# A graph network on one core: the edge loop's fill in another order, edge one-hots compared in bf16 with the tile innermost, Wq and Wk by chunks

## What is computed

```
L0: q, k, v = x@Wq+bq, x@Wk+bk, x@Wv+bv          # 8 heads of 64
    attention over the nodes, masked by the adjacency of the edges, softmax over the queries (axis 1)
    @Wo + bo, layernorm, relu(h@W1+b1)@W2+b2, layernorm
L1: h   = mish(concat(x[src], x[dst], edge_attr) @ W1 + b1)     # 4096 x 512
    m   = mish(h @ W2 + b2)                                     # 4096 x 512
    agg = segment_sum(m, dst);  u = mish(concat(x, agg)@W3 + b3);  u@W4 + b4;  layernorm
L2: two graph convolutions 512 -> 128 -> 512 with a normalised adjacency
L3: x@W_self.T + mean over neighbours(x)@W_neigh.T + bias, layernorm
```

## Time and profile before

| | |
|---|---|
| three runs | 254.29, 254.63, 255.37 us; median 254.63 |
| profiled execution | 255.16 us, its span 253.4 us, mean granted TensorE clock 0.977 |
| busy us (share of the span) | PE 235.5 (93%), PEld 189.6 (75%), DVE 153.9 (61%), ACT 121.6 (48%), POOL 5.6 (2%) |
| chain that ended last | PE 82%, DVE 8%, issue 4%, ACT 4%, POOL 1% |
| largest lines on it | L625 33%, L610 12%, L432 8%, L441 5%, L488 4% |

### The profile page before, as it was taken

How to read it: one execution, slowest core, us unless ns; L and a number is a source line. 1 busy time by engine, 2 the same in 40 slices (tenths; PEclk the granted TensorE clock), 3 DMA queues, 4 the chain that set the end, 5 groups by cost and what they waited for, 6 DMA issues and landing times.

```text
span 253.4 us, 3283 instructions
## 1 busy us (share of the span) xinstructions
PE 235.5 (93%) x1269; PEld 189.6 (75%) x1269; DVE 153.9 (61%) x266; ACT 121.6 (48%) x221; POOL 5.6 (2%) x17
## 2 busy tenths in 40 slices
PE   7998999997998499999999999999999998999980
PEld 3967789764765378888888888888888887986760
DVE  3977875336877335585675856758568355264625
ACT  0415399779267614553654735647455343150000
POOL 0000100001000000000000000000000000000001
PEclk9999999999999679999999999999999999999996
DMA  6999983501930000004505031040000000000001
GB/s 214 319 415 414 406 319 132 168 0 35 281 101 0 0 0 0 3 0 134 197 3 166 0 111 60 0 166 0 0 3 0 0 0 0 3 0 0 3 0 43
DMA packets 12991, 23.39 MB, mean 92 GB/s; under 512 B 920, under 2 KB 3888, under 8 KB 12848
## 3 DMA queue, kind: packets, MB, share of 16 engines
q1 hardware_dynamic: 12336, 22.81, 25.7%
q10 hardware_dynamic: 640, 0.37, 0.6%
HBM read 22.92 MB, written 0.26 MB: 91 GB/s over the span
## 4 chain that ended last, share of the span: by engine, by line
PE 82%; DVE 8%; issue 4%; ACT 4%; POOL 1%; POOLq 0%; DVEq 0%
PE bank L625 33%; PE bank L610 12%; PE bank L432 8%; PE bank L441 5%; PE bank L488 4%; PE bank L635 3%; PE bank L636 3%; PE bank L451 2%; ACT C L281 2%; DVE Sbf L829 2%; DVE Dbf L829 2%; PE bank L421 1%; PE bank L646 1%; PE bank L463 1%; PE bank L415 1%
## 5 line engine op out<-in xcount | busy, mean ns | idle before, releaser
L625 PE MATMUL bank<-W2hi,Hhi 128*128 128x512 f32 x128 | 51.1, 399 | 4.2 <-issue 4.2
L625 PE MATMUL bank<-W2lo,Hhi 128*128 128x512 f32 x128 | 50.9, 398 | 0.0
L625 PE MATMUL bank<-W2hi,Clo 128*128 128x512 f32 x128 | 50.8, 397 | 0.0
L365 ACT ACTIVATE Mhi<-M 128x512 fp32r<-128x512 f32 x32 | 20.2, 632 | 50.6 <-DVE M L933 50.6
L938 DVE TENSOR_TENSOR Mlo<-M,Mhi 128x512 fp32r<-128x512 f32 x32 | 22.1, 689 | 24.4 <-ACT M L366 24.4
L933 DVE TENSOR_TENSOR M<-bank,b2r 128x512 f32<-128x512 f32 x32 | 22.0, 687 | 17.8 <-PE bank L625 9.2
L625 PEld LDWEIGHTS bank<-W2hi,Hhi 128*128 128x128 f32 x128 | 24.7, 193 | 9.8 <-issue 4.6
L625 PEld LDWEIGHTS bank<-W2hi,Clo 128*128 128x128 f32 x128 | 24.7, 193 | 5.2
L625 PEld LDWEIGHTS bank<-W2lo,Hhi 128*128 128x128 f32 x128 | 24.7, 193 | 5.2
L358 ACT ACTIVATE Hhi<-C 128x512 fp32r<-128x512 f32 x32 | 20.0, 624 | 14.7 <-DVE C L919 14.4
L924 DVE TENSOR_TENSOR Clo<-C,Hhi 128x512 fp32r<-128x512 f32 x32 | 22.0, 688 | 6.6 <-ACT C L359 6.5
(11 more groups left out here) (178 smaller groups left out, 315.9 us busy)
## 6 DMA issues: line engine op xcount, KB each, us to landing
F<-in_L_gnn_W SPq DMA_DIRECT2D x2, 2048.0 KB, 13.3
W1raw<-in_L_gnn_W SPq DMA_DIRECT2D x1, 2048.0 KB, 20.9
W<-in_L_gnn_W SPq DMA_DIRECT2D x1, 2048.0 KB, 8.9
Wq<-in_L_gnn_Wq SPq DMA_DIRECT2D x2, 512.0 KB, 5.0
Wk<-in_L_gnn_Wk SPq DMA_DIRECT2D x2, 512.0 KB, 7.7
Wv<-in_L_gnn_Wv SPq DMA_DIRECT2D x1, 1024.0 KB, 11.8
ea<-in_edge_attr SPq DMA_DIRECT2D x1, 1024.0 KB, 12.5
Wo<-in_L_gnn_Wo SPq DMA_DIRECT2D x1, 1024.0 KB, 15.3
```

What stands on the lines that cost most here:

```text
L365: act.activation(Mhi[:, t, :], M[:, t, :], ACT.Mish)
L625: done = mm(ST2[t][:, :], x[:, c, e], w[:, c, :], start=c == 0 and i == 0, stop=c == KC - 1 and i == 2)
```

## The change

Four things are changed.

1. The one-hots. POOL fills a table `numbers` (128 x 128 nodes x 32 tiles, bf16) with the node number; DVE casts the ids to bf16 and compares in that layout, so that in `Dbf` and `Sbf` the 32 tiles lie next to each other for each node. The PE's operands `[:, :, t]` take every 32nd element. All 32 matmuls of `count_edges` stand behind V.
2. Wq and Wk are loaded in four chunks of rows each, and `features_as_loaded` multiplies a chunk into all four quarters as it arrives.
3. Ahead of the fill: edge step 5 moves ahead of the last part of F2's product; ACT's `W2hi` moves behind step 11; DVE's four pieces of `W2lo` are spread; `xw` (y plus a bias row) moves back; the load of W1raw goes behind three rows.
4. The fill. ACT and DVE take their work in another order, and the wait for the late banks moves into `second_layer`: six reads for tiles 0 and 1, eight for tiles 2 and 3.

```
+            pool.iota(numbers, pattern=[[1, N], [0, ET]], base=0, channel_multiplier=0,
+                      allow_small_or_imprecise_dtypes=True).then_inc(S["numbered"], 1)
...
-            for ids, one in ((dcol, Dbf), (scol, Sbf)):
-                v.tensor_tensor(one, ids[:, :].unsqueeze(2).to_broadcast([P, ET, N]),
-                                iota_row[:, :].unsqueeze(1).to_broadcast([P, ET, N]), ALU.is_equal).then_inc(S["onehot_bf"], 1)
+            v.tensor_copy(dcol_bf[:, :], dcol[:, :]).then_inc(S["ids_bf"], 1)
+            v.tensor_copy(scol_bf[:, :], scol[:, :]).then_inc(S["ids_bf"], 1)
+            dve.wait_ge(S["ids_bf"], 2)
+            dve.wait_ge(S["numbered"], 1)
+            for ids, one in ((dcol_bf, Dbf), (scol_bf, Sbf)):
+                v.tensor_tensor(one, ids[:, :].unsqueeze(1).to_broadcast([P, N, ET]), numbers, ALU.is_equal).then_inc(S["onehot_bf"], 1)
...
-                        done = mm(quarter(b, i), by_edge[:, tile_of(g, i), :], ident_bf[:, :], start=True, stop=True)
+                        done = mm(quarter(b, i), by_edge[:, :, tile_of(g, i)], ident_bf[:, :], start=True, stop=True)
...
-            for h in range(2):
-                pe.wait_ge(S[f"wq_in{h}"], 16)
-                features_by(bank[2], 0, (2 * h, 2 * h + 1), Wq, xT, KC, S["q_done"] if h else None)
+            def features_as_loaded(banks, w, arrived, signal):
+
+                per = KC // len(banks)
+                for c in range(KC):
+                    pe.wait_ge(S[f"{arrived}{c}"], 16)
+                    for j in range(KC):
+                        done = mm(quarter(banks[j // per], j), w[:, c, P * j:P * (j + 1)], xT[:, c, :],
+                                  start=c == 0 and j % per == 0, stop=c == KC - 1 and j % per == per - 1)
+                        if c == KC - 1 and j % per == per - 1:
+                            done.then_inc(signal, 1)
...
-                    done = mm(bank[0][:, 0:N], Dbf[:, t, :], Sbf[:, t, :], start=t == 0, stop=t == ET - 1)
+                    done = mm(bank[0][:, 0:N], Dbf[:, :, t], Sbf[:, :, t], start=t == 0, stop=t == ET - 1)
...
-            pe.wait_ge(S["onehot_bf"], 2)
-            count_edges(range(8))
             pe.wait_ge(S["qk_ready"], 2 * KC)
...
             nodes_by(bank[3], xT, Wv, S["v_done"])
-            count_edges(range(8, ET)).then_inc(S["ct_done"], 1)
+            pe.wait_ge(S["onehot_bf"], 2)
+            count_edges(range(ET)).then_inc(S["ct_done"], 1)
...
-            edge_term(range(3, 5))
+            edge_term(range(3, 6))
             for h in range(2):
                 columns_by((bank[1], bank[2]), ffT, F2, h, range(FC - 2, FC), 0, FC - 1).then_inc(S["f2_done"], 1)
 
-            edge_term(range(5, RING_STEPS - 1))
+            edge_term(range(6, RING_STEPS - 1))
...
                     if g >= 1:
                         pe.wait_ge(S["z2_read"], GT * (g - 1) + t + 1)
+                    else:
+                        pe.wait_ge(S["late_read"], 6 if t < 2 else 8)
...
             pe.wait_ge(S["w2_lo"], KC)
-            pe.wait_ge(S["late_read"], 2 * KC)
```

More of the change, by code:

```diff
@@ L63, in gnn_kernel @@
         scol = sb("scol", [P, ET], I32)
+        dcol_bf = sb("dcol_bf", [P, ET], BF16)
+        scol_bf = sb("scol_bf", [P, ET], BF16)
         Ahat = sb("Ahat", [P, N])
@@ L115, in gnn_kernel @@
         EAThi, EATlo = chunks(first["EAThi"], PAIRS), chunks(first["EATlo"], PAIRS)
-        Dbf, Sbf = chunks(other["Dbf"], ET), chunks(other["Sbf"], ET)
+        Dbf, Sbf, numbers = (other[n].rearrange("p (n t) -> p n t", t=ET) for n in ("Dbf", "Sbf", "numbers"))
         W1hi, W1lo = chunks(other["W1hi"], 2 * KC), chunks(other["W1lo"], 2 * KC)
@@ L204, in _ @@
             sp.dma_start(xs[:, :], a["x"]).then_inc(S["x_in"], 16)
-            for h in range(2):
-                sp.dma_start(Wq[:, :, D // 2 * h:D // 2 * (h + 1)], w_view(a["L0_gnn_Wq"])[:, :, D // 2 * h:D // 2 * (h + 1)]).then_inc(S[f"wq_in{h}"], 16)
-            for h in range(2):
-                sp.dma_start(Wk[:, :, D // 2 * h:D // 2 * (h + 1)], w_view(a["L0_gnn_Wk"])[:, :, D // 2 * h:D // 2 * (h + 1)]).then_inc(S[f"wk_in{h}"], 16)
+            for c in range(KC):
+                sp.dma_start(Wq[:, c, :], a["L0_gnn_Wq"][P * c:P * (c + 1), :]).then_inc(S[f"wq_in{c}"], 16)
+            for c in range(KC):
+                sp.dma_start(Wk[:, c, :], a["L0_gnn_Wk"][P * c:P * (c + 1), :]).then_inc(S[f"wk_in{c}"], 16)
             load_row("L0_gnn_bo")
@@ L216, in _ @@
             sp.dma_start(F1, w_view(a["L0_gnn_W1"])).then_inc(S["f1_in"], 16)
-            sp.dma_start(W1raw, w_view(a["L1_gnn_W1"][0:2 * D, :])).then_inc(S["w1_in"], 16)
             for name in EARLY_ROWS[4:]:
                 load_row(name)
+            sp.dma_start(W1raw, w_view(a["L1_gnn_W1"][0:2 * D, :])).then_inc(S["w1_in"], 16)
             sp.wait_ge(S["pre_done"], ST_UNIT)
@@ L347, in _ @@
             features_high(3)
-            edge_term_out(range(3))
+            edge_term_out(range(RING_STEPS))
             act.wait_ge(S["w2_in"], 16)
             act.activation(W2hi[:, :, :], W2raw, ACT.Copy).then_inc(S["w2_hi"], 1)
-            edge_term_out(range(3, KC * PAIRS - 3))
+            edge_term_out(range(RING_STEPS, RING_STEPS + 1))
             def hidden(g, j):
@@ L366, in message @@
                 act.activation(M[:, t, :], M[:, t, :], ACT.Mish).then_inc(S["m_hi"], 1)
-            for j in range(3):
+            for j in range(KC):
                 hidden(0, j)
[L370 to L377, removed]
+            edge_term_out(range(RING_STEPS + 1, KC * PAIRS))
+            for j in range(KC):
+                hidden(1, j)
             for g in range(G):
@@ L888, in _ @@
             v.tensor_copy(Cn[:, :], bank[4][:, N:2 * N]).then_inc(S["graph_ready"], 1)
+            dve.wait_ge(S["nx_ready"], 2)
+            chain(v.tensor_tensor(xw[:, :], y[:, :], r("L0_gnn_b2"), ALU.add))
             xb = r("L0_gnn_be2")
@@ L901, in _, with w2_low @@
             out_halves(xT_flat, xs_banks, S["nT_done"], 2, S["nT_ready"])
-            dve.wait_ge(S["w2_hi"], 1)
-            for c in range(KC):
-                v.tensor_tensor(W2lo[:, c, :], W2raw[:, c, :], W2hi[:, c, :].bitcast(F32), ALU.subtract).then_inc(S["w2_lo"], 1)
+            def w2_low(cs):
+                dve.wait_ge(S["w2_hi"], 1)
+                for c in cs:
+                    v.tensor_tensor(W2lo[:, c, :], W2raw[:, c, :], W2hi[:, c, :].bitcast(F32), ALU.subtract).then_inc(S["w2_lo"], 1)
             dve.wait_ge(S["ab_done"], 1)
@@ L946, in one_hot @@
                                 iota_row[:, :].unsqueeze(1).to_broadcast([P, GT, N]), ALU.is_equal).then_inc(S["m_oh"], 1)
[L948 to L955, removed]
+            for j in range(KC):
+                z1_out(0, j)
+            w2_low((2,))
+            for j in range(KC):
+                hidden_low(0, j)
+                z1_out(1, j)
+                if j == 0:
+                    w2_low((3,))
+            for j in range(KC):
+                hidden_low(1, j)
             for g in range(G):
```

15 lines of the change are left out of this document (7 added, 8 removed).

## The result

The changed kernel takes **258.9 us** (median of four runs, 258.07 to 259.85); the kernel before, on the same chip, 254.53. The ratio is 1.0167, 95% interval 1.0123 to 1.021: it is slower by 4.4 us, where 249.5 was forecast. The profiled execution took 258.64, its span is 256.8 us, the mean granted clock 0.977.

A forecast was written before the change was run, and what follows sets the result against it. The PE, busy 93% of the span, bounds the kernel where it waits or runs slow. -6.94 + 0.38 + 0.1 + 1.35 = -5.1 takes 255.16 to 250.05, median 249.5; range 247.6 to 253.4 (0.84).

The forecast's parts named there:

- Fill: Between `first_layer` and `second_layer`: the 4.19 us hole goes entirely, and the slow clock with it saves 2.75: -6.94 us.
- a wait in its place: Rival at the hole: `hidden_low(0,3)` or late z2 sums make a new wait, say 1.5 us: 251.0; chance 0.12.
- something misread: Rival at the hole: something misread holds the PE to 85 us anyway, only costs stay: 255 to 256; chance 0.04.
- Ring: Edge terms behind the second feed-forward product: step 5 ahead of F2's last part delays the PE's transposes: +0.38 us.
- W1raw at nothing: W1raw's load, 2.0 us later behind three rows, covered by 1.76 us idle ahead of step 1: 0 to 0.24, taken 0.
- Front, +0.1: Q, K and scores: K's last chunk closes all four quarters together, so scores start at 14.9, not 14.82: +0.1 us.
- cover for Wv: Wv's load behind four more issues, 0.1 us of cover before V: nothing to +1.9 us, taken as nothing.
- the table rival: Rival at the start: VectorE's identity waits for POOL's new iota, everything 3.2 us later: 252.7; chance 0.05.
- +1.35: Count behind V: strided moving reads at 0.115 us each, count ends at 23.35, its two products at 25.2: +1.35 us.
- the upper bound of 0.23: Most a strided moving read in the count would cost, from a record reading 512 columns: 0.23 us each, +5.0 us.
- That rival: Rival in the count: moving reads four times slower, +5.0 us, total -1.5, so 253.1; chance 0.16.
- the rival with both operands slow: Rival in count and one-hot transposes: both operands slow; at four times today's cost +7.9 us, 262.5; chance 0.08.

The follow-up runs named there:

- run 11: Kernel before with only the reordered fill, plus the load of W1raw issued behind the bias rows: 248.63 us.
- run 1: Changed kernel with the one-hots of the kernel before, all 32 count matmuls still behind V: 249.29 us.
- run 2: Changed kernel with GpSimd's table iota waiting until VectorE has made its identity: 255.67 us.
- run 5: Kernel of run 1 with W1raw issued ahead of the bias rows again: 249.31 us.
- run 6: Kernel of run 5 with the edge steps as before, two ahead of the first hidden product, not three: 249.01 us.
- run 12: Kernel before with the reordered fill, plus Wq and Wk by chunks and all count matmuls behind V (kernel of run 6 again): 249.03 us.
- run 7: Changed kernel with both identities made by `tensor_tensor` in place of `tensor_scalar`, the iota where the change put it: 256.05 us.
- run 8: Kernel of run 1 with 6 x 16 probe matmuls ahead of the count, moving operand at steps of 2 to 64 bytes: one run, 264.63 us.
- run 4: Changed kernel with only Sbf, the count's moving operand, in the new strided layout and Dbf as before: 257.75 us.
- run 3: Changed kernel with only Dbf, the count's stationary operand, in the new strided layout and Sbf as before: 252.48 us.

## Why the prediction was wrong, point by point

**Fill: right.** -7.24 in the traces against -6.94, hole and slow clock both; alone it gives 6.9 us by the medians, 7.2 by the spans (253.4 to 246.2). The slow clock had cost 3.01 rather than the 2.75 worked out from its 14 matmuls. The two rivals in it (a wait in its place, something misread) didn't occur; the slack on VectorE was 0.66 for 0.6.

**Ring: right.** +0.38 forecast, +0.56 to 0.57 measured, by the cause named (fewer steps ahead of ACT at the end). W1raw at nothing came true by luck: in the changed kernel the late front hid the load, and ACT never waited for it. The cover that was named is real but short: 1.0 us of waiting cost nothing in run 11, 2.1 us cost 0.9 in run 1. And the load was not 2.0 us later: it had landed at 33.6 before, and came at 36.3 (run 11), 36.98 (run 1) and 37.6 (changed kernel).

**Front, +0.1: right as to K's copies** (in run 2, with Q and K at the times of before, the scores start at 14.75 on PE's timeline, as before), too low in its cover for Wv. "A load that spends 11.8 us on its way is waiting for the bytes ahead of it" is borne out in part: issued 1.6 us later it spent 10.5 on its way instead of 11.8. What was missed is that with 0.1 us of cover every late landing of Wv counts (runs 2, 5, 6 and 12, and 11 with halves).

**The step that failed first: "Against: the identity's `tensor_scalar` shows 0.29 and a `tensor_tensor` of the same shape 0.28", and with it the 0.05 for the table rival.** Equal durations were taken as evidence that the identity uses no mode that the iota could block. They are none: the `tensor_scalar` took 0.29 in the kernel before and 4.17 beside the iota, run 7's `tensor_tensor` 0.29 beside it. Price: 3.2 forecast for that rival, 3.49 in the chain of the changed kernel. The iota took 4.17 us and not the 3.2 scaled from the small ones, the identity ended 3.88 later (5.41 against 1.24 + 0.29), and V started 3.49 later. Runs 2 and 7 win back 3.2 and 2.9.

**The second: "+1.35", the moving read at 0.115 us.** It was taken as twice the packed price from an f32 record with twice the bytes per column. The bytes that matter are those from column to column, 64 here, and the flat part of the curve in run 8 was reached: 217 to 218 ns alone (runs 4 and 8), 229 with the stationary operand strided too, the upper bound of 0.23. That bound came from a packed record with four times the columns, and no row had a strided read: that it fits so well is luck. That rival had 0.16, with +5.0 for its read; +6.38 was measured. The missing 1.4 is the clock, which no case had: 1.71 + 1.53 for the two products behind the count, instead of 1.84. Without it, 7.34 + 1.84 - 4.20 = +4.98. Runs 3 and 4 put both parts on the moving side; the rival with both operands slow fell (Sbf's transposes went from 0.45 to 0.50 to 0.52 per 8, not by a factor).

**The structure of the chances.** The two failures were rivals, with prices close to what came, but each was priced alone against a forecast that held the rest. With both, -6.94 + 0.48 + 5.0 + 3.2 = +1.7 would have been slower than before; their conditions had nothing to do with each other, but both were guesses at an edit that the trace of before could not show. With fill and ring right, the error is these two and the clock: 3.49 + (6.38 - 1.35) = 8.5 of the 9.4 us between forecast and result. Between the profiled executions it is 8.5 of 8.6 (258.64 - 250.05); the other 0.8 is the step from profiled to median, taken as -0.5 and found to be +0.26.

## What to carry to other kernels

A layout chosen so that one engine writes fast is read by another. Of the steps tried, keep the moving operand of a bf16 matmul within 4 bytes from column to column (58 ns, against 115 at 8 bytes), and let only a stationary operand be strided where its load is hidden. Keep a long GpSimd instruction (the iota, 4.17 us) away from the short VectorE operations on which the start depends, or write those in a form that it does not block; their duration when alone doesn't tell which form that is. And a bundle of edits can hide a clean gain of 7 us under a loss of 10: price each alone before keeping them together, since here the reordered fill alone was the whole gain.

## What the runs showed of the chip that was not expected

- The granted clock fell to 0.50 while TensorE was busy without a gap, during strided reads (the changed kernel, runs 2, 4, 7 and 8; in run 7 it was 0.50 from 24.3 to 27.4 us with TensorE busy for 3.10 of 3.10); in run 3, with the same count at packed moving reads, it stayed at 1.00. A busy share of 100% in the profile is thus no sign that the clock will hold. That slow reads are the reason is what these runs have in common; nothing else was varied to test it.
- The moving read costs 56, 58, 115, 226, 232, 218 ns for 128 bf16 columns at steps of 2, 4, 8, 16, 32, 64 bytes, the 16-byte step (run 8) and the 64-byte step (run 4) at either clock alike.
- A GpSimd iota of 4096 bf16 numbers per partition takes 4.17 us, and a 128-column `tensor_scalar` issued 0.09 us after it ends 4.17 us later than it starts, with no reader or writer in common.
